# Bias addition and weight sums moved behind the outputs of the first seven-product group in each layer of a GNN kernel

## The reference

```python
for i in range(L):                       # L = 4
    a = _attn(_ln(h, ln2_w[i], ln2_b[i]), cond, Wq[i], Wk[i], Wv[i], Wo[i])
    h = h + a
    u = _ln(h, ln3_w[i], ln3_b[i]) @ geglu_w[i] + geglu_b[i]
    val, gate = jnp.split(u, 2, axis=-1)
    f = val * jax.nn.gelu(gate, approximate=False)
    h = h + f @ ffo_w[i] + ffo_b[i]
```

## Time and profile before

| | us |
|---|---|
| median of 3 executions | 2404.89 (2403.44 to 2405.4) |
| profiled execution, whole | 2403.8 |
| its span in the profile | 2402.0 |
| TensorE busy (share of the span) | 2357.3 (98%) |
| VectorE busy | 1660.0 (69%) |
| ScalarE busy | 1118.0 (47%) |
| GpSimd busy | 668.9 (28%) |

### The profile page before, as it was taken

One profiled execution on the slowest core, in us unless ns is written; L12 is line 12 of the kernel. 1 busy time (PEld: TensorE's weight loads), 2 busy tenths in 40 slices (PEclk: granted clock), 3 DMA queues, 4 the chain that ended last, 5 costly groups with the idle time before them and its releaser, 6 DMA issues.

```text
span 2402.0 us, 32703 instructions
## 1 busy us (share of the span) xinstructions
PE 2357.3 (98%) x11951; PEld 1956.3 (81%) x11951; DVE 1660.0 (69%) x3177; ACT 1118.0 (47%) x2206; POOL 668.9 (28%) x439
## 2 busy tenths in 40 slices
PE   6899999999999999999999999999999999999999
PEld 4358888888888888888888888888888888888887
DVE  9986767785566766785566766785566766785554
ACT  9954444554334444554334444554334444554332
POOL 3111000066540000066540000066540000066540
PEclk9999999999999999999999999999999999999999
DMA  2031100122211100122211100122210100122222
GB/s 79 19 127 41 36 29 26 36 68 75 66 60 36 36 24 30 36 67 75 66 62 36 36 23 32 36 67 75 66 61 36 36 22 32 36 68 75 66 101 86
DMA packets 83307, 124.99 MB, mean 52 GB/s; under 512 B 5905, under 2 KB 63889, under 8 KB 78289
## 3 DMA queue, kind: packets, MB, share of 16 engines
q1 hardware_dynamic: 82864, 118.75, 15.0%
q10 hardware_dynamic: 288, 4.19, 0.4%
HBM read 116.36 MB, written 6.55 MB: 51 GB/s over the span
## 4 chain that ended last, share of the span: by engine, by line
PE 89%; DVE 5%; ACT 3%; issue 1%; POOL 1%; DMA 0%; SPq 0%; DVEq 0%; ACTq 0%; POOLq 0%
PE ps L2025 19%; PE ps L2026 19%; PE ps L2027 19%; PE ps L2365 7%; PE ps L2369 7%; PE ps L2367 7%; PE ps L2272 2%; PE ps L2289 2%; PE ps L2291 2%; DVE oh_d L1503 1%; PE ps L2286 1%; PE ps L2564 1%; DVE oh_d L1392 1%; PE ps L2161 1%; PE ps L2162 1%
## 5 line engine op out<-in xcount | busy, mean ns | idle before, releaser
L623 POOL TENSOR_TENSOR rstd<-veps,mhalf 128x1 f32<-128x1 f32 x48 | 26.0, 543 | 892.8 <-DVE veps L1293 892.8
L724 POOL TENSOR_TENSOR f_lo<-ff,f_hi 128x512 fp32r<-128x512 f32 x128 | 169.1, 1332 | 157.4 <-ACT f_hi L1183 157.3
L1956 DVE TENSOR_TENSOR h<-h,ps 128x512 f32<-128x512 f32 x256 | 168.8, 684 | 63.2 <-PE ps L2027 62.6
L975 ACT ACTIVATE v_hi<-ps 128x512 fp32r<-128x512 f32 x128 | 76.7, 599 | 284.8 <-PE ps L2027 284.8
L2025 PE MATMUL ps<-cond_hi,w_hi 128*128 128x512 f32 x512 | 202.1, 395 | 0.0
L2025 PE MATMUL ps<-w_hi,cond_hi 128*128 128x512 f32 x512 | 200.8, 392 | 0.0
L2025 PE MATMUL ps<-wf_hi,f_hi 128*128 128x512 f32 x512 | 199.6, 390 | 0.9 <-DVE ff L1940 0.8
L2027 PE MATMUL ps<-w_hi,cond_lo 128*128 128x512 f32 x512 | 200.3, 391 | 0.0
L2026 PE MATMUL ps<-cond_lo,w_hi 128*128 128x512 f32 x512 | 200.1, 391 | 0.0
L2027 PE MATMUL ps<-cond_hi,w_lo 128*128 128x512 f32 x512 | 200.1, 391 | 0.0
L2026 PE MATMUL ps<-w_lo,cond_hi 128*128 128x512 f32 x512 | 199.9, 390 | 0.0
(11 more groups left out here) (327 smaller groups left out, 6441.0 us busy)
## 6 DMA issues: line engine op xcount, KB each, us to landing
stage<-in_pieces SPq DMA_DIRECT2D x82, 512.0 KB, 3.3
stage<-in_condT SPq DMA_DIRECT2D x31, 1024.0 KB, 4.8
stage<-in_pieces SPq DMA_DIRECT2D x224, 128.0 KB, 2.6
at_s<-at_hi ACTq DMA_DIRECT2D x2, 2048.0 KB, 8.3
at_hi<-at_s SPq DMA_DIRECT2D x4, 1024.0 KB, 6.8
x<-in_x SPq DMA_DIRECT2D x2, 1024.0 KB, 6.8
out<-h SPq DMA_DIRECT2D x8, 256.0 KB, 2.0
bias_row<-in_rows SPq DMA_DIRECT2D x6, 256.0 KB, 3.8
```

Source lines behind the costliest of these rows:

```text
L724: pool.tensor_tensor(f_lo[q % 2][:, c, half * HALF:(half + 1) * HALF], ff[:, s % 2, :], bits(f_hi[q % 2][:, c, half * HALF:(half + 1) * HA ...
L1956: dve.tensor_tensor(h[:, t, :], h[:, t, :], ps[:, down_bank(q, t), :], ALU.add)\
```

## The change

In group 1, the first with a set of seven products, VectorE's `add_bias(NT - 1)` moves from ahead of the sums of `set_first(1, 1)` to behind them, and `weight_sums(2, 0)` moves from ahead of `set_last(1, 1)` to behind it. On ScalarE `sums_high(2, 0)` moves behind the second GELU of set (1, 1). The other groups keep their order, and no instruction is added or removed.

```diff
@@ -1240,10 +1240,12 @@
                     if q + 1 < MG:
                         blocks_high(q + 1, 0)
                     set_gelu(q, 1, 0)
-                    if q + 1 < MG:
+                    if 1 < q < MG - 1:
                         sums_high(q + 1, 0)
                     f_high(q, 2, 1, 1)
                     set_gelu(q, 1, 1)
+                    if q == 1:
+                        sums_high(q + 1, 0)
                     f_high(q, 3, 0, 1)
@@ -1988,15 +1990,19 @@
                 for e in range(2):
                     full_set(e)
-                add_bias(NT - 1)
                 for q in range(1, MG):
                     if q > 1:
                         set_first(q, 0)
                         set_last(q, 0)
                     set_first(q, 1)
-                    if q + 1 < MG:
+                    if q == 1:
+                        add_bias(NT - 1)
+                        set_last(q, 1)
                         weight_sums(q + 1, 0)
-                    set_last(q, 1)
+                    else:
+                        if q + 1 < MG:
+                            weight_sums(q + 1, 0)
+                        set_last(q, 1)
                     add_down(q - 1, range(3))
```

## The result

The changed kernel takes 2429.44 us (median of 4 executions, 2428.6 to 2430.43), the kernel before 2404.16 in the same session. The ratio is 1.0104, 95% interval 1.0092 to 1.0116: slower by 25.3 us, where 23.2 were forecast. The span of the profiled execution is 2427.5 us.

The account below looks back on a forecast made before the run. At set (2, 0) VectorE's chain already ends together with TensorE's product, without slack. Chain 16.4 us plus slow clock 6.8 gives 23.2 on 2404.9, so 2428 us; range 2416 to 2434, about 8 in 10.

Parts of the forecast that it names:

- The bias costs nothing: Bias moved behind the three sums of set (1, 1): lands at about 516 in VectorE's idle time, cost nothing.
- The outputs come 0.80 us earlier: Set (1, 1), layer 0: L1935 starts 0.12 us behind the first GELU, at 521.97, 0.80 us earlier; layer 3 1.16.
- The chain behind them: Sums (2, 0) 4.49 us late delay set_low(2, 0), sums (2, 1), additions four and five; TensorE loses 4.3 us in layer 0.
- Two of four sums blocked: Sums (2, 1): two wait for GpSimd's f_low; loss 4.3 us in layer 0; with one slow stretch a layer, chance 0.45.
- The lower rivals (one or none): Sums (2, 1): one blocked loses 3.2 us in layer 0, none 2.2; 2413 to 2424 us in all; chance 0.2.
- the queueing read at 505 us: Rows of 505 to 510 us: small two-input VectorE operations and GpSimd's alternate, one instruction each; VectorE's take 1.65 and 2.61 us.
- The sum over the layers: Chain loss of 4.3 us in layer 0 and 3.9 in layer 3, over four layers 16.4 us.
- The clock: TensorE behind the pause before set (2, 0): one slow stretch at 1.2 GHz, 1.7 us a layer, 6.8 in all.
- the rival with two slow stretches in each layer: Behind the pause before set (2, 0): clock costs 3.4 us a layer, 30 us slower in all, 2435 us; chance 0.08.
- The rival without a loss by the clock: Pause before set (2, 0): two sums blocked, no clock loss, 2421.3 us; chance 0.2.
- Nothing later gives it back: From 531.53 on TensorE releases nearly all; the loads shift by 4.5 us with everything else.
- Not slower: Rival: outputs win 0.80 us in layer 0, up to 1.16 in layer 3, 3.9 in all: 2401 us; chance 0.04.

Follow-up runs that it names:

- with GpSimd out of the way: Changed kernel with GpSimd's two f_low of group 1 moved behind set_low(2, 1): 2416.61 us, ratio 1.0052.
- the pause filled: Changed kernel with 20 unused matmuls more per layer, issued by TensorE in the pause ahead of set (2, 0): 2420.54 us, ratio 1.007.
- two runs that gave 2406: Changed kernel with eight additions ahead of sums (2, 1): 2406.43 us; the same plus the attention-weight split moved behind ScalarE's block-product copy: 2406.54 us.

## Why the prediction was right, point by point

- **The bias costs nothing.** Right. It lies in idle time, and alone it gives 1.0003.
- **The outputs come 0.80 us earlier.** Right in mechanism, and in layers 0 and 3 in size (0.78 and 1.23 us). L1937 starts 0.09 us behind the end of the GELU (520.53 + 0.71 = 521.24, then 521.33). Between the same two points, the end of the DMA's wait on ScalarE and L1940, before needs 4.64 us (520.39 to 525.03) and the changed kernel 3.80 (519.78 to 523.58), 0.84 less. In layer 2 the load came 0.9 us later and only 0.05 us were left; that the load comes at the same time was assumed.
- **The chain behind them.** Right link by link: first sum (2, 0) to set_low 1.63 us (1.64 forecast), set_low to f_low 4.19 (4.17), VectorE idle 2.55 us in front of the sums (2, 1), last additions to TensorE 1.43 (1.43).
- **Two of four sums blocked.** Right. The lower rivals (one or none) fall: the two sums take 1.47 and 1.48 us, the four 3.58 us in all (3.60 forecast), and with GpSimd out of the way 1.47. It was the step with the widest range, and the queueing read at 505 us settled it. The lock held for a whole instruction, which the Trainium skill states ("SBUF — State Buffer", section "SBUF: two separate sides"), agrees with these sums of 1.47 and 1.48 us; that the engines alternate is from the rows alone.
- **The sum over the layers.** 16.4 us forecast; 17.1 in the changed kernel by the start of set (2, 0), 16.7 by the layers' lengths with the pause filled. Layers 0 and 3 are as forecast (4.27 for 4.3, 3.81 for 3.9). The forecast drew a line between them; layer 1 has 4.07 and layer 2 has 4.99, by its late load.
- **The clock.** The mechanism was right and the size too small: 1.7 us a layer forecast, 9.0 to 9.7 in all or about 2.4 measured. The term took the stretch behind the pause of 141.78, 3.6 us long. After the pauses of 5 us the slow stretch has about that length in layer 1 alone (3.4 us). In the other three it is 6.8 to 6.9 us long, and 0.7 to 2.3 us of it lie inside the pause and cost nothing. So the rival with two slow stretches in each layer had the length right in three layers of four, but its price of 3.4 us a layer was reached in none (2.9 in layer 2 is nearest to it). In all the clock took some 2.5 us more than forecast and the chain 0.7 more, while the changed kernel's layers began 0.66 us earlier in the profile; the medians differ from the forecast by 2.1. The rival without a loss by the clock falls by the run with the pause filled.
- **Nothing later gives it back.** Right.
- **Not slower.** Its condition, set_low(2, 0) 3 us earlier and additions free of it, was met by moving the GELUs and the additions. Of the runs made only that one shows the outputs' gain, 5.0 us where I had allowed 3.9. The outputs were freed of the DMA too there. Whether the kernel before would gain the same by these two moves, without the change, was not run.

What the prediction did not see is the second half of the damage: the sums (2, 1) are also on the way of the next group's copies and loads. It didn't matter for its number, since TensorE's start shifted everything, but it made me expect 2401 and then 2404 for two runs that gave 2406.

## What to carry to other kernels

Before an instruction is moved behind another to free that one, follow what hangs on the moved one: here four sums of 1.5 us in all were the head of a chain through another engine and back into the mover's own queue, and 4.4 to 5.3 us of delay at its head were 3.8 to 5.0 us of TensorE's time in each layer. A single buffer or counter that links two steps on different engines makes such a chain. Where the engine at the end is the bound, its clock can add to a pause: here 9 to 10 us on pauses of 19.9. And a gain of under 1 us at one wait was real here only when the waits behind it were moved too: the change with both other edits gave 5 us, the change alone or with one of them a loss, and the additions alone nothing. The GELUs alone were not run.

## What the runs showed of the hardware

Small VectorE operations with two inputs in SBUF that are queued against back-to-back GpSimd operations passed one at a time, each behind a whole GpSimd operation: 0.41 us became 1.47. When the queue on GpSimd's side ended, they were back at 0.41.

TensorE's clock after a pause between dense products is not a matter of the pause's length alone: four pauses of 2.66 us in one execution were followed by 1.2 GHz three times, four of 2.6 to 2.9 us in another twice, and eight of 4.2 to 5.0 us each time. The four that were filled with matmuls whose results nobody reads never were. Nor did the slow stretch have one length: in the changed kernel it lasted 3.4 us in one layer and 6.8 to 6.9 us in three. What decides either is not shown here.
